# Other places within 128 bytes for the matmul operands of a graph-attention layer

## The reference

```
u     = x @ x.T / sqrt(384);  p = softmax(u);  delta = p * adj
attn  = delta / (sum(delta, -1) + 1e-10)
h_w   = x @ W_w.T + b_w                      for w = left, self, right
ctx   = attn[j > i] @ h_left + diag(attn) * h_self + attn[j < i] @ h_right
o     = relu(layernorm(ctx, eps 1e-12) * gamma + beta)
out   = layernorm(x + o, eps 1e-5)
```

## Time and profile before

| | before |
|---|---|
| median of three runs | 465.34 us (465.21 to 465.38) |
| the profiled execution, whole | 466.12 us |
| its span, first to last instruction | 464.4 us |
| granted TensorE clock, mean | 0.996 |
| busy: PE, PEld | 97%, 96% of the span |
| busy: DVE, ACT, POOL | 82%, 69%, 45% of the span |
| matmuls | 2633 |
| DMA | 80.20 MB, mean 173 GB/s |

### The profile page before, as it was taken

The page is one execution under the profiler, slowest core; times in us unless marked ns, Lnnn a source line. Parts: engine busy times, 40 slices in busy tenths (PEclk is TensorE's granted clock), DMA queues, the critical chain, the costliest instruction groups (busy, mean ns, idle before and its releaser), DMA issues.

```text
span 464.4 us, 9444 instructions
## 1 busy us (share of the span) xinstructions
PE 452.5 (97%) x2633; PEld 448.1 (96%) x2633; DVE 382.2 (82%) x1115; ACT 322.4 (69%) x714; POOL 209.4 (45%) x294
## 2 busy tenths in 40 slices
PE   8999999999999999999999999999999999999992
PEld 6999899999999999999999999999999999999981
DVE  4767988889888879888888888878988888888866
ACT  6673786776776776677767678677677777666752
POOL 0105455443455543445543345554344554344552
PEclk9999999999999999999999999999999999999998
DMA  8546466655555664555665556566555566544311
GB/s 258 184 119 196 139 195 195 193 169 180 175 181 181 215 192 137 180 186 176 202 192 180 160 165 195 181 193 192 156 170 189 172 215 192 158 161 151 99 68 68
DMA packets 83862, 80.20 MB, mean 173 GB/s; under 512 B 7042, under 2 KB 76164, under 8 KB 83844
## 3 DMA queue, kind: packets, MB, share of 16 engines
q1 hardware_dynamic: 83840, 79.98, 54.7%
q10 hardware_dynamic: 4, 0.00, 0.0%
HBM read 51.65 MB, written 28.31 MB: 172 GB/s over the span
## 4 chain that ended last, share of the span: by engine, by line
PE 85%; DVE 5%; ACT 3%; POOL 2%; DMA 2%; issue 2%; SPq 1%; POOLq 0%; DVEq 0%
PE ps_proj L456 55%; PE ps_ctx L491 19%; PE ps_scores L448 3%; PE ps_scores L442 2%; PE ps_scores L444 2%; PE ps_scores L405 2%; DMA dt_raw<-dt_dram 2%; ACT normed L599 1%; POOL rstd L1017 1%; SPq L306 1%; DVE y_sb L818 1%; PE ps_ctx L412 1%; ACT ps_scores L550 1%; DVE stats L785 1%; POOL shifted L1027 0%
## 5 line engine op out<-in xcount | busy, mean ns | idle before, releaser
L456 PE MATMUL ps_proj<-w_hi,xt_split 128*128 128x384 f32 x1152 | 304.9, 337 | 0.9 <-ACT ps_proj L569 0.9
L456 PEld LDWEIGHTS ps_proj<-w_hi,xt_split 128*128 128x128 f32 x1152 | 209.3, 188 | 1.6 <-ACT ps_proj L569 1.6
L456 PE MATMUL ps_proj<-w_lo,xt_split 128*128 128x384 f32 x576 | 193.6, 336 | 0.0
L1017 POOL TENSOR_TENSOR rstd<-var_eps,minus_half 128x4 f32<-128x4 f32 x32 | 36.2, 1130 | 188.8 <-DVE var_eps L804 186.3
L456 PEld LDWEIGHTS ps_proj<-w_lo,xt_split 128*128 128x128 f32 x576 | 108.3, 188 | 0.0
L569 ACT ACTIVATE ps_proj<-bias 128x384 f32<-128x384 f32 (+1 forms) x192 | 92.6, 494 | 5.2 <-DVE proj_lo L770 4.9
L1023 POOL TENSOR_TENSOR scaled<-normed,gamma_sb 128x384 f32<-128x384 f32 x62 | 63.1, 1018 | 37.6 <-ACT normed L599 31.7
L573 ACT ACTIVATE proj_hi<-ps_proj 128x384 fp32r<-128x384 f32 x128 | 63.5, 497 | 9.1 <-PE ps_proj L456 8.8
L770 DVE TENSOR_TENSOR proj_lo<-ps_proj,proj_hi 128x384 fp32r<-128x384 f32 x128 | 67.4, 545 | 2.7 <-ACT proj_hi L573 2.7
L593 ACT ACTIVATE ps_ctx<-ps_proj,diag 128x386 f32<-128x386 f32 x64 | 35.7, 557 | 45.8 <-PE ps_proj L456 45.8
L1027 POOL TENSOR_TENSOR shifted<-scaled,beta_sb 128x384 f32<-128x384 f32 x62 | 63.5, 1024 | 2.4
(11 more groups left out here) (84 smaller groups left out, 628.6 us busy)
## 6 DMA issues: line engine op xcount, KB each, us to landing
x_sb<-in_x SPq DMA_DIRECT2D x32, 384.0 KB, 4.5
xt_sb<-in_x_t SPq DMA_DIRECT2D x31, 384.0 KB, 3.9
out_dram<-out_sb SPq DMA_DIRECT2D x31, 384.0 KB, 2.9
adj_sb<-in_adj SPq DMA_DIRECT2D x32, 256.0 KB, 4.6
dt_dram<-turned SPq DMA_DIRECT2D x31, 256.0 KB, 2.0
dt_raw<-dt_dram SPq DMA_DIRECT2D x124, 64.0 KB, 2.0
cross_dram<-cross_turned SPq DMA_DIRECT2D x29, 256.0 KB, 2.0
cross_raw<-cross_dram SPq DMA_DIRECT2D x116, 64.0 KB, 2.0
```

What stands on the lines that cost most here:

```text
L456: mm = nc.tensor.matmul(ps_proj[bank(at, g)][:, 0:H], stationary, moving[w][:, c, :], start=False, stop=True, skip_group_check=True)
L1017: nc.gpsimd.tensor_tensor(rstd[at.slot(2)][:], var_eps[:], minus_half[:], ALU.pow).then_inc(rstd_ready, 1)
```

## The change

It adds a helper that allocates an unused pad of 8 float32 (32 bytes) for each partition ahead of a tensor, and uses it ahead of w_hi1 and w_hi2, of all three w_lo and of all four xt_split. It widens the rows of proj_hi and proj_lo from 386 to 392 columns, of which the last six are not used: `attend` takes columns 0 to 385. Instructions, their number, their order and their waits are the same; only addresses differ.

```diff
--- before.py
+++ after.py
@@ -89,6 +89,7 @@
     BANK = 512
     ONE = H
     HE = H + 2
+    ROW = H + 8
 
     R = 32
     Q = P // R
@@ -115,8 +116,14 @@
         zeros = sb("zeros", [P, HE], F32R)
         minus_half = sb("minus_half", [P, 2 * T])
         w_raw = [sb(f"w_raw{w}", [P, C, H]) for w in range(3)]
-        w_hi = [sb(f"w_hi{w}", [P, C, H], F32R) for w in range(3)]
-        w_lo = [sb(f"w_lo{w}", [P, C, H], F32R) for w in range(3)]
+
+        def off_by(name, lines, shape):
+            if lines:
+                sb(f"pad_{name}", [P, 8 * lines])
+            return sb(name, shape, F32R)
+
+        w_hi = [off_by(f"w_hi{w}", min(w, 1), [P, C, H]) for w in range(3)]
+        w_lo = [off_by(f"w_lo{w}", 1, [P, C, H]) for w in range(3)]
         bias = [sb(f"bias{w}", [P, HE]) for w in range(3)]
         gamma_sb = sb("gamma_sb", [P, H])
         beta_sb = sb("beta_sb", [P, H])
@@ -126,7 +133,7 @@
         xt_sb = [sb(f"xt_sb{i}", [P, C, L]) for i in range(UNROLL)]
         adj_sb = [sb(f"adj_sb{i}", [P, T, L]) for i in range(UNROLL)]
 
-        xt_split = [sb(f"xt_split{i}", [P, C, 2 * L], F32R) for i in range(UNROLL)]
+        xt_split = [off_by(f"xt_split{i}", 1, [P, C, 2 * L]) for i in range(UNROLL)]
         z_sum = [sb(f"z_sum{i}", [P, T]) for i in range(2)]
         diag = [sb(f"diag{i}", [P, T]) for i in range(2)]
         y_sb = [sb(f"y_sb{i}", [P, T, H]) for i in range(2)]
@@ -149,8 +156,9 @@
         dt_left = sb("dt_left", [P, 2, T, P], F32R)
         dt_right = sb("dt_right", [P, 2, T, P], F32R)
 
-        proj_hi = sb("proj_hi", [P, NSPLIT, HE], F32R)
-        proj_lo = sb("proj_lo", [P, NSPLIT, HE], F32R)
+
+        proj_hi = sb("proj_hi", [P, NSPLIT, ROW], F32R)
+        proj_lo = sb("proj_lo", [P, NSPLIT, ROW], F32R)
 
 
         stats1 = sb("stats1", [P, T, 6])
@@ -486,7 +494,7 @@
                 for which, blk, g in ATTEND[t]:
                     pe.wait_ge(proj_lo_ready, at.n(NSPLIT, g + 1))
                     hi, lo = (from_[which][:, half, blk, :] for half in range(2))
-                    m_hi, m_lo = proj_hi[:, g, :], proj_lo[:, g, :]
+                    m_hi, m_lo = proj_hi[:, g, 0:HE], proj_lo[:, g, 0:HE]
                     for s, m in ((hi, m_hi), (hi, m_lo), (lo, m_hi)):
                         mm = nc.tensor.matmul(ps_ctx[:, t, 0:HE], s, m, start=False, stop=True, skip_group_check=True)
                 mm.then_inc(ctx_ready, 1)
```

## The result

The changed kernel takes 469.75 us (median of four runs, 469.53 to 470.03); the kernel before, run beside it, 465.36 us (465.21 to 465.89). The medians are 4.4 us apart; the ratio is 1.0088, with a 95% interval of 1.0073 to 1.0103, which is 3.4 to 4.8 us: slower, clear of noise. The profiled execution took 469.53 us with a span of 467.8 us, against 466.12 and 464.4 before.

The account below looks back on a forecast made before the run. TensorE, busy 97%, was taken as the bound: matmul count times pace. Profiled 466.1 us + 0 for projections - 0.3 for attention = 465.8, less 0.8 to the timed median: 465.0 us; range 461.0 to 469.5.

Parts of the forecast that it names:

- What bounds the kernel: Whole run: TensorE, busy 97% of the span; time is matmul count times pace, plus a head and a tail.
- the choice of zero for the projections: The 1728 projection matmuls: new operand places cost 0 us, the value shared by the two distances on record.
- the same place costs nothing extra: Score matmuls, both operands at one place, carry the projections' 13.3 ns on top; so being apart cannot cause 173.3 ns.
- the 162.5 ns: Projection pace by the skill page's gap formula for 384 columns, N/2.4 + 2.5 ns; the trace shows 173.3.
- The bounds: Projections, two distances not shown, half of 1728 matmuls: between -11.5 us and +3.4 us.
- the slow rhythm: Second matmul pace seen in the first 36 projections: 177.2 ns against 173.3, 3.9 ns more.
- the whole 13.3 ns: Projection time above 160.0 ns of columns; if gone for 864 matmuls, -11.5 us.
- The slower rival: Matmuls fall into a pace 3.9 ns slower as places change: +6.7 us if always, +1.7 for a quarter; chance 0.27.
- The attention: 192 triples of 386 columns: proj rows at multiples of 32 gain -0.3 us in all, bounds -1.6 to +2.2.
- What I said would show it: Changed kernel's chain: 7.80 per 45 projections in four batches is the forecast; differing batches mean distance; 7.95 in all, slower pace.
- The scores piece: Nine score matmuls of a batch: must stay at 1.24 us; a change would mean absolute place matters, not distance.
- The faster rival: Projections: a read clash, cheaper at an unseen distance; -5.7 us for a quarter, -11.5 for half; chance 0.18.

Follow-up runs that it names:

- e5: Kernel before with all four xt_split slots at 64 modulo 128, the same place as all weights: 469.50 us, ratio 1.0080.
- e6: Kernel before with all xt_split slots at 96 modulo 128, all weights staying at 64: 471.31 us, ratio 1.0119.
- e1: Kernel before with only the weight halves at the changed kernel's places (w_hi 64, 96, 0; w_lo 32, 64, 96): 469.58 us, ratio 1.0076.
- e4: Kernel before with all w_lo moved to 96 modulo 128, all w_hi staying at 64: 467.85 us, ratio 1.0033.
- e13: Kernel before with w_hi and w_lo at (64, 96, 64) modulo 128, each pair in fact 128 apart modulo 256: 469.01 us, ratio 1.0065.
- e3: Kernel before with only dt, proj_hi and proj_lo as in the changed kernel (at 0, rows of 392 columns): 466.91 us, ratio 1.0012.
- e2: Kernel before with only the four xt_split slots at the changed kernel's places (96, 0, 32, 64): 467.78 us, ratio 1.0034.
- e14: Kernel before with weights at 192 modulo 512 and xt_split slots at distances 0, 32, 64, 288: 466.59 us, one time.
- e16: Kernel before with weights at 192 modulo 512 and xt_split slots at distances 448, 480, 96, 128: 467.12 us, one time.
- e15: Kernel before with weights at 192 modulo 512 and xt_split slots at distances 320, 352, 384, 416: 468.62 us, one time.
- e18: Changed kernel with each w_lo moved to its w_hi's place modulo 512, the rest kept: 468.59 us, ratio 1.0056 to the kernel before.
- e17: Kernel before with proj rows of 512 columns at 288 and dt at 480 modulo 512, attention at distance 192 throughout: 466.52 us, ratio 1.0005.
- e8: Kernel before with proj rows of 416 columns at 0 and dt at 96, modulo 128: 467.12 us, ratio 1.0034.

## Why the prediction was wrong

**What bounds the kernel** held. TensorE's count times pace is the time; no wait grew, and the work of the other engines at new places stayed hidden, as costed.

**The step that failed** is the choice of zero for the projections. It rested on the sentence that the same place costs nothing extra, drawn from the score matmuls, and from it that distance can't matter; measured, the term is +3.8 us. Three things were wrong with it. The places were counted modulo 128 because the change is described so; the period is 256. And of eight distances modulo 256 the trace of before showed the projections at one and the scores at another, both among the six fast ones: two like values out of eight were read as a law. e5 and e6 show the missing two, +3.8 and +5.6 us when a whole kernel has them. And it priced each pair by itself, as if a mixture cost the mean of its parts: e1, with no slow distance in it, is 1.0076 times the kernel before, so the mixture is the larger part of the error.

The prediction also named a rule by which this term is zero, the independent read ports for weight loads and moving operands ("TensorE: Matmul & The Clock Gate", "Step-by-step: what each phase is for", of the Trainium skill). The measurement decides against what was drawn from it: places alone took the projections from 173.3 to 176.7 ns (e6). Whether the two reads clash no run shows. And the 162.5 ns that it held against the trace come from a formula that the Trainium skill ("TensorE: Matmul & The Clock Gate", "Back-to-back issue gap") gives for an isolated matmul, not for a stream with a weight load before each, so the trace's 173.3 ns don't contradict it; no steady piece of projections came near 162.5.

**The bounds** of the term were -11.5 and +3.4 us, and the measured one lies just above. The upper end, half of the projections at 3.9 ns more, came from the slow rhythm of the earlier trace rows; measured are 2.2 ns on all 1728, which is 3.8 us. That the two nearly agree is luck, as twice the matmuls pay little more than half the price. The lower end, the whole 13.3 ns going, was seen nowhere: in no layout did a steady projection fall below 173.3.

**The slower rival** was the truth in kind: a rhythm that doesn't hold when places change from one matmul to the next. What it named is what e1, e4 and e13 show. It had a chance of 0.27. The upper end of the whole range, 469.5, is 0.25 us too low: it held the 3.9 ns for half to three quarters of the projections, and what came is 2.2 ns on all of them.

**The attention** was put at -0.3 us from the hundredths of the earlier trace rows; e3 has +0.6 us (1.0012, interval from 1.0000), within the bounds of -1.6 to +2.2 but of the other sign, and in the changed kernel the piece is 3.18 to 3.20. Here rows at a multiple of 32 bytes aren't better than rows at 8 modulo 16.

**What I said would show it** did in part: more than 7.80 in a single batch means distance (e2). The slow rhythm was to show as 7.95 or more in all batches; the changed kernel has 7.88 to 7.91 in all, which is neither sign. The scores piece, which was to stay at 1.24, did: it is 1.24 or 1.25 in both kernels.

**The faster rival** has nothing for it: no distance of the eight runs below 173.3. Still open is a rule for mixtures: counted pair by pair, slow distances are 30 of the 216 projections of four batches in the changed kernel, 30/216 x 1728 x 3 ns = 0.7 us (an estimate; 3 ns lies between the prices of 128 and 160), and its slot 2 has none and is as slow as the rest (7.90). The remaining 3.1 of the 3.8 us are mixture and what ran before; how much is each wasn't separated, and what in TensorE or SBUF makes these rhythms no run here tells.

## What to carry to other kernels

When TensorE is the bound, take the pace of its matmuls from start to start and compare it with columns over clock: a few nanoseconds each can be a matter of where the operands lie. Keep operands that take turns within a group of matmuls, such as the halves of a split operand, at the same place modulo 512 bytes, as here, and let no pad shift one of them alone. Count the distance between stationary and moving operand modulo 256, and keep it off 128 and 160. Buffers of a ring may differ if all their distances are fast (e14: 7.80 and 7.81 in all four slots). An even row pitch was no gain in itself here. All this is measured on 384 columns of float32r with a weight load before each.

## What the runs showed of the hardware that I had not expected

The pace of a 384-column float32r matmul with a weight load before it goes by the distance between its operands modulo 256 bytes: 173.3 to 173.8 ns at six of eight distances in steps of 32, 175.6 to 176.0 at 128 and 176.7 at 160 (e2, e5, e6, e14 to e16). Fast distances mixed within triples ran at 174.4 to 175.3 ns (e4, e13, e1). The same distance at the same places modulo 512 ran at 173.3 or 176.7 ns in different kernels (e15 against e18). At 2.4 GHz, the level granted here, 173.3 and 176.7 ns are 416 and 424 cycles. And the attention, with its places untouched modulo 256, took 3.16 or 3.18 us in e2 and 3.19 in e1, and with other rows 3.17 (e17) to 3.21 (e8).
